# CIN kernel, one core: the transposes of the next group's x directly behind the product with the block-diagonal fields of tile 1

## What is computed

```
x_vec = input                                    # (512, 64, 16)
for W, b in ((W0, b0), (W1, b1), (W2, b2)):
    z = einsum('bhd,bfd->bhfd', x_vec, input)    # every pair of a row of x_vec and a field
    z = z.reshape(B, h * f, d)
    x_vec = einsum('oc,bcd->bod', W, z) + b[None, :, None]
    outs.append(x_vec.sum(axis=2))
return concatenate(outs, axis=1)                 # (512, 384)
```

## Time and profile before

| | |
|---|---|
| median of 3 runs | 1140.29 us (1138.67 to 1140.75) |
| time of the profiled execution | 1139.53 us |
| span of its instructions | 1137.7 us |
| mean granted TensorE clock | 0.991 |
| TensorE busy | 1096.1 us (96%) |
| VectorE busy | 868.1 us (76%) |
| ScalarE busy | 453.2 us (40%) |
| GpSimd busy | 840.5 us (74%) |

### The profile page before, as it was taken

One profiled execution on the slowest core, in us unless ns is written; L12 is line 12 of the kernel. 1 busy time (PEld: TensorE's weight loads), 2 busy tenths in 40 slices (PEclk: granted clock), 3 DMA queues, 4 the chain that ended last, 5 costly groups with the idle time before them and its releaser, 6 DMA issues.

```text
span 1137.7 us, 16831 instructions
## 1 busy us (share of the span) xinstructions
PE 1096.1 (96%) x4589; PEld 775.6 (68%) x4589; DVE 868.1 (76%) x3002; ACT 453.2 (40%) x1532; POOL 840.5 (74%) x762
## 2 busy tenths in 40 slices
PE   2899999999999999999999999999999999999996
PEld 2477666676668666666668666766667766766776
DVE  3356978888794888979794797978887588888991
ACT  2244434444341443434352343434443253443550
POOL 3766796979784797878876688787978479697551
PEclk9989999999999999999999999999999999999998
DMA  7861423314051141514142051423313133240000
GB/s 248 249 165 40 93 72 68 91 27 123 24 122 44 34 115 23 124 35 112 54 93 56 17 115 51 95 70 72 94 29 102 35 81 85 41 111 15 1 1 28
DMA packets 112350, 86.89 MB, mean 76 GB/s; under 512 B 75136, under 2 KB 75776, under 8 KB 112128
## 3 DMA queue, kind: packets, MB, share of 16 engines
q1 hardware_dynamic: 109376, 75.27, 27.6%
q10 hardware_dynamic: 2880, 10.55, 2.6%
HBM read 14.75 MB, written 0.79 MB: 14 GB/s over the span
## 4 chain that ended last, share of the span: by engine, by line
PE 83%; DVE 11%; DMA 3%; issue 2%; POOL 1%; ACT 0%; SPq 0%; POOLq 0%
PE y L644 54%; PE l L656 19%; DVE acc L584 8%; PE xt L679 5%; PE l2p L691 3%; DMA xg<-in_r_input_dram 2%; DVE bd L551 2%; DMA z<-xg 1%; DVE x1l L559 1%; PE l2p L668 1%; PE xt L661 1%; PE y L733 0%; PE l L652 0%; POOL z L337 0%; DVE acc L582 0%
## 5 line engine op out<-in xcount | busy, mean ns | idle before, releaser
L584 DVE SCALAR_TENSOR_TENSOR acc<-y,x0t,acc 128x128 f32<-128x128 f32 x2560 | 699.2, 340 | 201.6 <-PE y L644 198.9
L490 ACT ACTIVATE prod<-y,x0t 128x128 f32<-128x128 f32 x1280 | 367.6, 371 | 607.0 <-PE y L644 573.8
L644 PE MATMUL y<-w1h,x1h 128*128 128x512 f32 x1024 | 509.3, 497 | 6.2 <-DVE acc L584 4.3
L644 PE MATMUL y<-w1h,x1l 128*128 128x512 f32 x1024 | 404.3, 395 | 0.0
L644 PE MATMUL y<-w1l,x1h 128*128 128x512 f32 x1024 | 403.7, 394 | 0.0
L348 POOL TENSOR_TENSOR pacc<-pacc,prod 128x512 f32<-128x512 f32 x192 | 247.1, 1287 | 183.8 <-ACT prod L490 183.8
L337 POOL TENSOR_TENSOR z<-z,xg 128x512 f32<-128x512 f32 (+1 forms) x272 | 353.0, 1303 | 25.7 <-DMA z<-xg 25.5
L644 PEld LDWEIGHTS y<-w1h,x1h 128*128 128x128 f32 x1024 | 193.4, 189 | 136.5 <-issue 60.3
L656 PE MATMUL l<-z,w0t 128*128 128x512 f32 x512 | 262.6, 594 | 2.7 <-POOL z L337 2.7
L644 PEld LDWEIGHTS y<-w1l,x1h 128*128 128x128 f32 x1024 | 193.6, 189 | 81.1 <-issue 54.3
L644 PEld LDWEIGHTS y<-w1h,x1l 128*128 128x128 f32 x1024 | 192.6, 188 | 44.1
(11 more groups left out here) (50 smaller groups left out, 278.4 us busy)
## 6 DMA issues: line engine op xcount, KB each, us to landing
z<-xg SPq DMA_DIRECT2D x512, 128.0 KB, 2.4
xg<-in_r_input_dram SPq DMA_DIRECT2D x32, 128.0 KB, 3.8
w2t<-in_L_rec_W_dram ACTq DMA_DIRECT2D x8, 512.0 KB, 12.4
gram<-in_L_rec_W_dram ACTq DMA_DIRECT2D x8, 512.0 KB, 8.6
z<-xg SPq DMA_DIRECT2D x16, 192.0 KB
gram<-in_L_rec_W_dram ACTq DMA_DIRECT2D x1, 2048.0 KB, 7.9
out_dram<-z SPq DMA_DIRECT2D x4, 192.0 KB, 2.1
b1r<-in_L_rec_b_dram ACTq DMA_DIRECT2D x1, 64.0 KB, 10.0
```

The costliest lines, as they stand in the source:

```text
L490: last = nc.scalar.activation(prod[:, h % HSLOTS, k, :], y[c % YB][:, k * O:(k + 1) * O], ACT.Copy, scale=x0t[:, j, f:f + 1])
L584: ins = nc.vector.scalar_tensor_tensor(out=to, in0=of, scalar=x0t[:, j, f:f + 1], in1=b1r[:] if m == 0 else to, op0=ALU.mult, op1=ALU.add)
L644: ins = nc.tensor.matmul(to, stationary, moving, start=(first and k == 0), stop=(last and k == 2))
```

## The change

One number of the hand-written order is another one. `LAYER2_AT` is 12 and `CHUNKS` is 16, so the transposes move from step 30 to step 28, which is the step of tile 1 in which `layer2` stands.

```diff
-TURN_AT = 30
+TURN_AT = LAYER2_AT + CHUNKS
```

## The result

The changed kernel takes 1134.99 us (median of 22 runs, 1133.1 to 1139.61), the kernel before 1140.47 us (22 runs, 1138.06 to 1143.55). The ratio is 0.9958, 95% interval 0.9948 to 0.9967: 0.42% faster, forecast were 0.39%. It is not the quotient of the two medians, which would be 0.9952. Four runs of the changed kernel that follow each other took 1138.74 to 1139.61 us at a granted clock of 0.988, the other 18 took 1133.1 to 1137.01 us at 0.989 to 0.994, and no reason for the four is known.

A forecast was written before the change was run, and what follows sets the result against it. TensorE's instruction order was taken to bound the kernel. Saving 15 x 0.34 = 5.1 us less 0.7 us of stalls gives -4.4 us, so 1135.9 us against the median 1140.29; range 1134.4 to 1138.8 us with chance 0.85.

The forecast's parts named there:

- The passage: Between `layer2` and the transposes: one passage out of and one into the 64-row form go, 0.34 us per group, 15 groups.
- The upper of the two ends: First transpose starts 0.22 behind `layer2`'s second pair, its load hidden; 0.34 us per group goes, 5.1 us in all.
- the lower end: First transpose held 0.32 behind `layer2`'s second pair, its load exposed; only 0.19 us per group goes, 2.85 us in all.
- Rival 1: Behind `layer2`, the first transpose's load is held, so only 2.85 - 0.7 = 2.2 us goes, 1138.1 us; chance 0.2.
- Rival 2: Between `layer2` and transposes, changing operand form costs as much as the two passages replaced; 1139 to 1141 us; chance 0.09.
- The stall: Ahead of chunk 28 in groups 4, 8 and 12, the earlier wait makes it 0.23 us late, 0.7 us in all.
- Rival 3: VectorE carries the 0.25 us lateness of chunks 29 and 30 to each group's end; slower, 1144.7 us; chance 0.05.
- the anchor of 0.79: Near the group's end, before 311.76, VectorE waits 0.79 us for TensorE; unchanged if the forecast holds, gone if rival 3 does.

The follow-up runs named there:

- the upper rows: Against the kernel with the wait directly ahead of the transposes in step 28, transposes read the upper 64 partitions of `xg` and identity; 1133.97 us, ratio to before 0.9957.
- Taking the wait away: Against the changed kernel, the wait moved from ahead of chunk 28 to directly ahead of the transposes, behind `layer2`; 1134.95 us, ratio to before 0.9950.
- the wait alone: Against the kernel before, only the wait for `l2_used` and `x0t_made` moved ahead of chunk 28, transposes left in step 30; 1141.08 us, ratio 1.0012.

## Why the prediction was right

**The bound.** TensorE's order is the time: what was taken between its starts at the place is missing from the length of each group. The spans, 1137.7 and 1132.0, differ by 5.7 us. Of these 4.9 lie in groups 1 to 14; the rest is in group 0 and at both ends, which differ by as much from trace to trace.

**The passage.** Forecast 0.34 us per group at the place, measured 0.35; forecast 1.55 from last to second start, measured 1.54. The upper of the two ends held: the load was hidden. The prediction put 0.2 on the lower end, in part by a rule that its own already speak against (see "Which rows"). Rival 1 (0.19 and the load held) is out by the timeline of the changed kernel, and by the upper rows once more. Rival 2 (the passage between the two operand forms costs as much) is out by the same rows: 0.22 between pair and transpose.

**The stall.** Forecast 0.23 in each of three groups, measured 0.21; the load was to stand 0.06 behind the end of L445 and stands 0.07 behind it. Taking the wait away gave 0.21 back, the wait alone cost 0.23.

**VectorE.** The changed kernel's timeline of VectorE, which answers to the earlier trace rows:

```profile
288.75 2.16 DVE L584 SCALAR_TENSOR_TENSOR acc<-y,x0t,acc 128x128 f32<-128x128 f32 x8 [0.52 <-PE y L644]
...
292.36 0.87 DVE L584 SCALAR_TENSOR_TENSOR acc<-y,x0t,acc 128x128 f32<-128x128 f32 x3 [0.42 <-PE y L644]
...
309.46 0.87 DVE L584 SCALAR_TENSOR_TENSOR acc<-y,x0t,acc 128x128 f32<-128x128 f32 x3 [0.79 <-PE y L644]
```

The whole of this trace lies 1.91 earlier at the place (284.98 against 286.89), so 288.75 is 290.66 on the scale of before, which is the forecast. The accumulations of chunks 30 and 31 now stand in one piece, the idle stretch of 0.78 behind them is 0.42 (forecast 0.44), and the anchor of 0.79 at the end of the group is untouched. Rival 3 did not come about.

**What the sum left out.** The group is 0.40 us shorter, not 0.35. The other 0.05 lies behind the place. In the changed kernel chunks 31 and 32 of group 3 run at 0.226 us per matmul:

```profile
288.55 0.39 PE L644 MATMUL y<-w1h,x1h 128*128 128x512 f32 x1
...
289.68 0.39 PE L644 MATMUL y<-w1h,x1l 128*128 128x512 f32 x1
```

289.68 - 288.55 = 1.13 for five steps, where five at 0.23 make 1.15. The prediction had taken every step at 0.23, so this term is missing from its sum. Over 14 whole groups, counted from group 1, the distances fell by 4.9 us: eleven times about 0.40, three times about 0.17. Group 0 should add 0.4, but its length differs by more than that from trace to trace (72.2 to 73.7 us). In all that is 5.3 us by the traces, where 4.4 were forecast; the steps of the chunks, 0.05 x 15 = 0.75, are most of the difference. The clock is coarser than this: 5.5 us between the medians, 4.8 by the ratio, and its interval runs from 3.8 to 5.9, with the forecast in it. Why the steps of these chunks are shorter than elsewhere was not tried and stays open.

## What to carry to other kernels

Where TensorE is the bound, read the distances between starts at every change of the row form (the `64*128` against `128*128` of a profile's rows): here each stretch of 64-row instructions between 128-row ones paid about a third of a microsecond for going in and out, whatever stood in it. Gather such pieces, or give a small one the full rows if the data allows. When a piece moves, its wait moves too: put the wait directly ahead of the instruction that needs it, not ahead of the work in front of it.

## What the runs showed of the hardware

- Going from 128-row to 64-row instructions and back cost 0.33 us beyond the transposes themselves (two places of 0.46 against one of 0.59), and of the load at either border 0.05 to 0.11 us was not hidden. Where 64-row instructions followed each other the load was hidden (first transpose 0.22 behind `layer2`'s pair); so it was where a 128-row transpose followed a chunk (0.23).
- A 64-row transpose in an open stretch added about 0.065 us (0.13 for two). Four 128-row transposes with twice the columns put 0.43 us between two chunks, less than four 64-row ones at 0.59.
- TensorE's sequencer ran ahead of the matmuls: before the change it had passed a wait 2.8 us before the chunk that the wait guards, and of the 3.43 us that it stood in one after the change only 0.21 us reached the matmuls.
